# Edge counts of a four-layer graph network: 16 steps per register load, and two chunks of counts loaded inside the build

## The reference

```
h = relu(layernorm(x))
x = x + L0(h)      # graph convolution, batch norm, relu
h = relu(layernorm(x))
x = x + L1(h)      # graph convolution, norm, silu, two-head attention, norm, silu
...
x = x + L2(h)      # five gated steps over the graph, then two dense layers
...
x = x + L3(h)      # eight-head attention, elu, one-head attention
```

```
xw = x @ W;  src, dst = edges + loops;  deg = segment_sum(ones, dst)
norm = deg**-0.5 [src] * deg**-0.5 [dst]
h = segment_sum(xw[src] * norm, dst) + b
```

## Time and profile before

| | us |
|---|---|
| median of three runs | 3403.79 (3402.35 to 3407.19) |
| the profiled execution, its own time | 3405.62 |
| its span, first to last instruction | 3403.8 |
| count stage, in the span | 37 to 332 |
| first convolution's matmuls | 340.3 to 421.2 |

### The profile page before, as it was taken

The page is one execution under the profiler, slowest core; times in us unless marked ns, Lnnn a source line. Parts: engine busy times, 40 slices in busy tenths (PEclk is TensorE's granted clock), DMA queues, the critical chain, the costliest instruction groups (busy, mean ns, idle before and its releaser), DMA issues. The chain is left out here.

```text
span 3403.8 us, 41036 instructions
## 1 busy us (share of the span) xinstructions
PE 2807.8 (82%) x13998; PEld 2155.1 (63%) x13998; DVE 1760.0 (52%) x4016; ACT 1368.7 (40%) x2596; POOL 961.7 (28%) x779
## 2 busy tenths in 40 slices
PE   5776977899998699999999999999844445446998
PEld 3333875577776578787877787877533334445775
DVE  7987765999977452111122112111534543356994
ACT  3565034699997221111111112111323333342896
POOL 6100043000000453232322231321177777750000
PEclk9977979899999799999999999999855555555999
DMA  4232633101100432121212121310242221113100
GB/s 135 100 101 88 263 130 155 39 40 40 44 1 1 192 150 97 58 92 68 87 63 90 65 92 57 116 70 1 74 141 47 46 46 38 29 21 126 78 35 20
DMA packets 79695, 266.66 MB, mean 78 GB/s; under 512 B 21129, under 2 KB 53344, under 8 KB 70176
## 3 DMA queue, kind: packets, MB, share of 16 engines
q1 hardware_dynamic: 62520, 236.50, 18.6%
q0 software_dynamic: 16976, 27.54, 3.7%
HBM read 232.80 MB, written 31.18 MB: 78 GB/s over the span
## 5 line engine op out<-in xcount | busy, mean ns | idle before, releaser
L2799 PE MATMUL psum<-gate_stream,parts 128*128 128x384 f32 (+1 forms) x3600 | 667.9, 344 | 16.9 <-POOL gate_stream L2872 12.5
L2799 PEld LDWEIGHTS psum<-gate_stream,parts 128*128 128x128 f32 x3600 | 631.5, 189 | 33.8 <-issue 14.4
L2872 POOL CAST gate_stream<-gate_adj 128x1920 fp32r<-128x1920 f16 (+1 forms) x200 | 371.1, 1863 | 851.3 <-PE psum L2799 828.2
L2153 PE MATMUL psum<-gat_h,gat_pair 128*128 128x129 f32 (+1 forms) x3750 | 571.1, 291 | 8.6 <-DVE gat_pair L1957 7.7
L2153 PEld LDWEIGHTS psum<-gat_h,gat_pair 128*128 128x128 f32 (+1 forms) x3750 | 461.5, 191 | 123.4 <-issue 77.7
L1485 POOL DMA_INDIRECT edge_rows<-edge_table,src_idx x440 | 431.7, 981 | 180.7 <-issue 133.7
L2890 DVE SCALAR_TENSOR_TENSOR gate_work<-psum,bhh,gate_work 128x384 f32<-128x384 f32 (+1 forms) x80 | 50.0, 626 | 793.7 <-PE psum L2762 763.1
L1957 DVE SCALAR_TENSOR_TENSOR gat_pair<-gat_above,gat_adj 128x512 f32<-128x512 f32 (+3 forms) x525 | 326.6, 622 | 86.8 <-PE psum L2153 56.7
L2066 ACT ACTIVATE gat_above<-psum,gat_as 128x512 f32<-128x512 f32 (+3 forms) x525 | 329.7, 628 | 41.4 <-PE psum L2141 39.9
L2057 ACT ACTIVATE psum<-gat_ad_rows,gat_as 128x512 f32<-128x512 f32 (+3 forms) x525 | 334.9, 638 | 16.9
L1912 DVE SCALAR_TENSOR_TENSOR gat_acc<-gat_adj,gat_q,gat_acc 128x512 f32<-128x512 f16 (+3 forms) x497 | 328.4, 677 | 0.0
(11 more groups left out here) (486 smaller groups left out, 3700.8 us busy)
## 6 DMA issues: line engine op xcount, KB each, us to landing
gate_adj<-adj SPq DMA_DIRECT2D x35, 2400.0 KB, 8.1
gat_adj<-adj SPq DMA_DIRECT2D x8, 3200.0 KB, 11.3
adj<-count_stage SPq DMA_DIRECT2D x196, 100.0 KB, 1.6
gcn_adj<-adj SPq DMA_DIRECT2D x8, 2400.0 KB, 8.2
edge_place<-row_scratch SPq DMA_DIRECT2D x40, 352.0 KB, 3.8
gate_adj<-adj SPq DMA_DIRECT2D x5, 2800.0 KB, 9.1
gcn_adj<-adj SPq DMA_DIRECT2D x4, 3200.0 KB, 10.0
edge_rows<-edge_table,src_idx POOLq DMA_INDIRECT x440
```

Of the source, the lines that this page charges most:

```text
L2153: mm = e.matmul(ps[0:p, b, a:a + D + 1], pair[:, g % 2, i * P:i * P + p], h1[:, hi, h, :], start=hi == 0 and i % 3 == 0, stop=hi == NT - 1 ...
L2799: mm = e.matmul(ps[:, f, 0:hi - lo], parts[:, t, m, f, :], stream[:, (NGG * i + t // GG) % GR, 0:windows(i), t % GG * W:(t % GG + 1) * W], ...
L2872: e.tensor_copy(stream[:, n % GR, 0:windows(i), :], cols[:, i % 2, 0:windows(i), g * GW:(g + 1) * GW]).then_inc(widened, 1)
```

## The change

It has three parts.

1. TensorE loads the registers of `RL` = 16 steps (32 registers) at once, where it loaded those of 4 steps (8 registers); `route_r` and `lowt` are padded to a multiple of 16 steps. ScalarE loads those of 14 windows, where it loaded 4.
2. The buffers `cols` and the two semaphores of their loads are made before the count stage. In it, the SP queue loads the first chunk behind the store of window 16 and the second behind that of window 40, each after waiting for the stores of all windows that the chunk reads. `gcn_first` issues no load for these two.
3. Six buffers of the tables and counts get their room in others that are not yet in use then: `wl` in `own`, `node_row` in `h`, `later` in `norms`, `near` in `parts`, and `key_f`, `low_f`, `low_i` in `folded`.

```diff
-LP = -(-BSTEPS // LS) * LS
+RL = 16
+LP = -(-BSTEPS // RL) * RL
-WL = 4
+WL = 14
...
-        wl = self.sb("wl", [P, LAYERS, 2, S2], F32, st)
+        wl = own[:, 0:4 * LAYERS, :].rearrange("p (l j a) w -> p l j (a w)", l=LAYERS, j=2)
...
-        key_f, low_f = sb("key_f", [BK, BJ, P]), sb("low_f", [BK, BJ, P])
-        low_i = sb("low_i", [BK, BJ, P], I32)
+        spare = fold[2][0:BK].rearrange("p b m w -> p (b m w)")[:, 0:3 * BJ * P].rearrange("p (k j w) -> p k j w", k=3, j=BJ)
+        key_f, low_f, low_i = spare[:, 0], spare[:, 1], spare[:, 2].bitcast(I32)
-        node_row = sb("node_row", [P, NP])
-        later = sb("node_later", [ER, 2, NP], BF16)
+        node_row = h[:].rearrange("p t w -> p (t w)")
+        later = norms[:].bitcast(BF16).rearrange("p (g n) -> p g n", g=2)
...
-        near = self.sb("node_near", [P, NT, SE], F32, st)
+        near = parts[:].rearrange("p t m w -> p t (m w)").bitcast(F32)
+        spans = self.gcn_spans()[0]
...
-                regs = [e.alloc_register(self.name("route_reg")) for _ in range(8)]
+                regs = [e.alloc_register(self.name("route_reg")) for _ in range(2 * RL)]
-                    if j % 4 == 0:
-                        e.load(regs, route[0:1, 2 * j:2 * j + 8])
+                    if j % RL == 0:
+                        e.load(regs, route[0:1, 2 * j:2 * (j + RL)])
-                    e.wait_ge(freed, need[j % 4])
-                    e.matmul(flat[:, bass.ds(at[j % 4], ROW)], low[:, j // LS % LRING, :, j % LS], hot[:, j % HRING, :],
+                    e.wait_ge(freed, need[j % RL])
+                    e.matmul(flat[:, bass.ds(at[j % RL], ROW)], low[:, j // LS % LRING, :, j % LS], hot[:, j % HRING, :],
...
                     e.dma_start(adj[:, w * ROW:(w + 1) * ROW], stage[:, w % SRING, :]).then_inc(stored[w % SRING], 16)
+                    for c, (lo, hi) in enumerate(spans[:2]):
+                        if w == hi // W + SRING:
+                            for s in range(SRING):
+                                e.wait_ge(stored[s], 16 * (hi // W // SRING))
+                            e.dma_start(cols[:, c, 0:(hi - lo) // W, :], self.adj[:, lo // W:hi // W, :]).then_inc(loaded[c], 16)
...
                     if c >= 2:
                         e.wait_ge(widened, NGG * (c - 1))
-                    e.dma_start(cols[:, c % 2, 0:(hi - lo) // W, :], self.adj[:, lo // W:hi // W, :]).then_inc(loaded[c % 2], 16)
+                        e.dma_start(cols[:, c % 2, 0:(hi - lo) // W, :], self.adj[:, lo // W:hi // W, :]).then_inc(loaded[c % 2], 16)
...
-        self.adjacency(h, own, parts, norms)
         cols = self.far("gcn_adj", [P, 2, GC // W, ROW], F16, inner)
+        loaded = [self.nc.alloc_semaphore(f"first_loaded{s}") for s in range(2)]
+        self.adjacency(h, own, parts, norms, cols, loaded)
```

More of the change, by code:

```diff
@@ L88 @@
 assert REAL % EG == 0 and REAL % 4 == 0 and ER * EPR == ET * P and REAL - KP < STEPS - KP < REAL
-assert ND >= N and BP >= BSTEPS and LP >= BP and NMC * MC == ND and NW % WL == 0
+assert ND >= N and BP >= BSTEPS and LP >= BP and RL % LS == 0 and NMC * MC == ND and NW % WL == 0
 class Chain:
@@ L536, in edge_places, with adjacency @@
         self.rows_last = far("rows_last", [8, STEPS])
-    def adjacency(self, h, own, parts, norms):
+    def adjacency(self, h, own, parts, norms, cols, loaded):
         nc = self.nc
@@ L560, in adjacency, with adjacency_tables @@
         self.adjacency_tables(ps, keyt, lowt, route_r, until_r, iota_hot, iota_low,
-                              (node, tile_i, before, dst_rows), (scale, shift), fold, first_w)
+                              (node, tile_i, before, dst_rows), (scale, shift), fold, h, norms, first_w)
         self.adjacency_counts(ps, keyt, lowt, route_r, until_r, iota_hot, iota_low,
-                              (node, tile_i, before, dst_rows), (scale, shift), fold, h, first_w, own, parts, norms)
+                              (node, tile_i, before, dst_rows), (scale, shift), fold, h, first_w, own, parts, norms, cols, loaded)
         st.close()
-    def adjacency_tables(self, ps, keyt, lowt, route_r, until_r, iota_hot, iota_low, nodes, norm, fold, first_w):
+    def adjacency_tables(self, ps, keyt, lowt, route_r, until_r, iota_hot, iota_low, nodes, norm, fold, h, norms, first_w):
         nc = self.nc
@@ L686, in _ @@
                 for g in range(2):
[L687 removed]
+                    inst = e.tensor_scalar(later[0:ER, g, :], node_row[0:ER, :], first_d[:, g:g + 1], None, ALU.is_gt)
                 inst.then_inc(compared, 1)
@@ L697, in _ @@
                 e.wait_ge(fetched, 16 * BJ)
-                e.tensor_scalar(low_i[:], rows[0:BK, :, :], P - 1, None, ALU.bitwise_and).then_inc(made, 1)
+                e.tensor_scalar(low_i, rows[0:BK, :, :], P - 1, None, ALU.bitwise_and).then_inc(made, 1)
                 e.wait_ge(made, 11)
@@ L725, in _ @@
                 e.wait_ge(made, 11)
-                e.copy(low_f[:], low_i[:]).then_inc(taken, 1)
+                e.copy(low_f, low_i).then_inc(taken, 1)
                 e.wait_ge(turned, 1)
@@ L750, in _ @@
                     for g in range(2):
-                        mm = e.matmul(ps[:, 7, t:t + 1], later[:, g, t * P:(t + 1) * P], one_bf[0:ER, :], start=g == 0, stop=g == 1)
+                        mm = e.matmul(ps[:, 7, t:t + 1], later[0:ER, g, t * P:(t + 1) * P], one_bf[0:ER, :], start=g == 0, stop=g == 1)
                 mm.then_inc(tiled, 1)
@@ L763, in adjacency_counts @@
     def adjacency_counts(self, ps, keyt, lowt, route_r, until_r, iota_hot, iota_low, nodes, norm, fold, h, first_w, own,
-                         parts, norms):
+                         parts, norms, cols, loaded):
         nc = self.nc
@@ L995, in gcn_spans, with gcn_first @@
         return spans, [[(t, min(P, hi - t * P)) for t in range(lo // P, -(-hi // P))] for lo, hi in spans]
-    def gcn_first(self, own, parts, norms, x1, stats, load, cols, stream, ahead):
+    def gcn_first(self, own, parts, norms, x1, stats, load, cols, stream, loaded, ahead):
         nc = self.nc
@@ L1013, in gcn_first @@
                 "given", "also"))
-        loaded = [nc.alloc_semaphore(f"first_loaded{s}") for s in range(2)]
         spans, tiles = self.gcn_spans()
@@ L2232, in load @@
             return 8
-        self.gcn_first(own, parts, norms, h, stats, load, cols, stream, ahead)
+        self.gcn_first(own, parts, norms, h, stats, load, cols, stream, loaded, ahead)
         first.close()
```

2 lines of the change are left out of this document (1 added, 1 removed).

## The result

| | before | changed kernel |
|---|---|---|
| median of the runs, us | 3403.79 (3402.35 to 3407.19) | 3441.72 (3437.31 to 3448.91) |
| ratio | 1 | 1.0111, interval 1.0096 to 1.0127 |
| profiled span, us | 3403.8 | 3440.1 |
| first to last weight load of the count steps, us | 38.3 to 330.2 | 40.1 to 371.9 |
| first convolution's first matmul, us | 340.29 | 376.87 |

The forecast was 3385, at most 3402. What came is rival (b)'s size (3433), though only part of it is (b)'s mechanism. The last row but one carries nearly all: 292.0 us of count steps became 331.7, 39.7 more. The first step came 1.8 us later, behind its longer first load, and from the last count step to the convolution's first matmul it is 5.0 us in place of 10.0. Together that is 36.6, the span's 36.3 but for 0.3.

What follows compares the result with a forecast made beforehand. No engine was full: ScalarE waited for TensorE, and TensorE for its own sequencer's register loads. The terms -27 + 8 + 1.5 + 1.5 - 3.4 made -18.4 us, from 3403.8 to 3385 us, range 3364 to 3402 (8 in 10).

Steps and rivals of the forecast that it cites:

- rival (b): Count stage, TensorE's wait for a freed bank: bursts pay copy and zeroing in full, +32 us, about 3433; chance 0.12.
- The load's price: TensorE's load of 32 registers at line 923: in proportion to the registers, 2.15 us.
- The moves: Register moves behind TensorE's load: between 0.15 and 0.78 us, middle 0.47 taken, with 0.13 of gaps.
- the 27: Count stage: 16 steps take 6.29 us against 7.00, 0.71 less, 38 times, so 27 us gained.
- my 0.87 us per load: Count stage before the change: of a 1.75 us period, load (0.59), moves (0.15) and gaps (0.13).
- So I charge nothing: Array at half clock in the count stage: 16 steps take at most 6.2 us, under 6.29, so no cost.
- The 20 folds ... have the load as their cover now: Folds of line 938: they still end under the 2.75 us gap, no cost; 31 us if cover were gone.
- VectorE's ring, +8: Ring of 8 steps between VectorE and TensorE: lumps of VectorE's work, 26 us, lose a third, 8 us given back.
- ScalarE's loads, 1.5: ScalarE's 14 loads of 14 registers: about 1.0 us each and hidden; 0 to 21 us possible, 1.5 taken.
- The loads in the build and the convolution: Chunks loaded early: TensorE loses 0 to 3 us in the build, 1.5 taken; the convolution starts 3.4 us earlier.
- The shared buffers: Part 3: same instructions on other addresses, no wait added, so nothing; a lost order costs a microsecond at most.
- the forecast's own range: Whole kernel, without rivals: 3373 (nothing given back) to 3396 (dear moves, 3 us each for ScalarE and DMA); chance 0.65.

Runs made afterwards that it cites:

- e9: e3 with the 20 folds issued every 16 steps from step 48, ahead of the register load, not every 12 from 40: 3420.12 us, ratio 1.0046.
- e6: e3 with ScalarE zeroing and freeing each window's bank right behind its copy, not one window later: 3422.7 us, ratio 1.0056.
- e3: The changed kernel with only ScalarE's register loads back at 4 windows, TensorE's kept at 16 steps: 3436.13 us, ratio 1.0086.
- e4: The changed kernel with longer rings, 15 steps of hots for 8 and 4 of lows for 3: 3438.06 us, ratio 1.0088.
- e1: The changed kernel with TensorE's loads back at 4 steps and ScalarE's at 4 windows, parts 2 and 3 kept: 3401.93 us, ratio 0.9989.
- both repairs: e6's and e9's edits together, against the kernel before: 3403.13 us at 16 steps in a load, 3391.36 us at 8.
- e5: e1 with the routing words as 16-bit integers, half the bytes of a load: 3606.54 us, ratio 1.0587.
- e10: e1 with one packed register a step instead of two, the bank worked out from its low bits: 3414.83 us, ratio 1.0028.

## Why the prediction was wrong, step by step

- **The load's price** was right: 2.36 us for the 2.15 taken. The moves were not: from the load's start to the first weight load the median is 3.52 us, so load, moves and gaps are 3.30 beyond a step's 0.22, where I had 2.75. 0.21 of the difference is the load, 0.34 are moves and gaps, 0.94 in all where I took 0.60 between 0.28 and 0.91. The dear end, four times the moves of one load of 8, was true; there was no ground for the middle. By these medians 16 steps take 6.84 us, which leaves 6 of the 27. In the stage not even these came: loads and plain steps took 244.4 us for 244.1. The kernel before's short loads hid part of the array's work at half clock, which my 0.87 us per load did not credit them with. That this is where the 6 us went is my reading and not shown.
- **"So I charge nothing"** for half clock: 18.7 us, the largest row. I held 6.2 us of array time for 16 steps against a 6.29 us period, as if the two could lie beside each other freely. They can't, since the load comes only behind the burst's issue, and at half clock the steps of a burst come 0.33 us apart, with 3.3 us of load behind. No experiment changed the clock alone; the 18.7 us are the sorting's.
- **"The 20 folds ... have the load as their cover now ... they still end under the 2.75 us gap."** They did not: all other matmuls cost 13.6 us more, the folds 8.2 of them. I treated cover as a property of the load's length, not of its place. Folds stand at steps 40 + 12n, all multiples of 4, so in the kernel before each came right behind a load, where it cost 0.95 us; only every fourth is a multiple of 16, and the other 15 landed inside bursts. It could be read in the code. Real cover came only with e9, which puts them ahead of the load: 16.0 us. My price for it ("Were that cover gone, 20 x 1.55 = 31 us would be lost") was twice that.
- **Rival (b)** was right in place and cause, but its price of 32 us was too high: 5.9 us more in the sorting, 13.4 by e6. With ScalarE's own loads, which hold the same chain, it is 19.0 (e3 and e6). That the total came near its 3433 is luck, since most of the loss was half clock, folds and the gain that failed. I asked whether ScalarE keeps its 0.81 us when fed, which it does from 222.88 on above; what I left out is that it can begin a burst late.
- **VectorE's ring, +8**: the longer ring of e4 gave 4 to 8 us back, with intervals that overlap, so the size may have held. The mechanism didn't: TensorE's chain had become the longer by far (VectorE idled 77.6 us before its hots, in place of the 32 in all that I named).
- **ScalarE's loads, 1.5**: 5.6 (e3), not clear of the noise. The bound given, 0 to 21, held; 14 registers in one load were nearer to the dear end.
- **The loads in the build and the convolution**, +1.5 - 3.4: e1 gave -3.7, so the first term was about 0.
- **The shared buffers**: nothing seen, but not tried apart; e1 has them too and isn't slower.

Of the sum, the term of 27 us came to nothing; two that stood at zero, half clock and folds with the features, made 32.3 us, and waits for a bank 5.9 on top. The range had no room for them: half clock had no upper bound at all, and the folds' 31 us stood in the text and in no case. The upper end of the forecast's own range does not follow from its terms either: 3403.8 - 15 + 8 + 3 + 3 - 3.4 is 3399, not 3396.

## What to carry to other kernels

Before loads or waits are merged into fewer and longer ones, price the long one against the sum of the short ones: here 95.4 us against 99.6, so there was next to nothing to gain. Then list what stood right behind each of the old ones and where it stands after. Work behind a load is not under it; put it ahead, and the load covers it once it is longer than the work. Give buffers back at once. Here 8 steps in a load with both repairs took 3391 us, where 16 without repairs took 3442 and 16 with them 3403. An operation "at no cost" in a sum needs an upper bound like any other.

## Of the hardware, not expected

- A sequencer's load from SBUF of 32-bit words takes longer nearly in proportion to the registers: 4 take 0.33 us, 8 0.59, 16 1.28, 32 2.36 (medians on TensorE), so merging saved little: four loads of 8 would be 2.37. Registers of 16-bit words cost 0.25 us each (e5).
- ScalarE's loads of 14 registers took from 1.2 to 3.4 us in one run, median 2.3, more than TensorE's of 16 (1.28). Whether the number or the engine makes it, no run shows.
- One AND and shift per step on TensorE's sequencer moved the steps from 0.22 to 0.33 us apart (e10).
- The same unchanged kernel took 3403 to 3406 us on three chips and 3717 to 3742 on three others, with pauses of all engines together that no view explains.
